# Wide cross-attention: a slot's order rewritten on TensorE, ScalarE and VectorE

## The chip, the cores and the metric

The kernel runs on one core of one Trainium2 chip. The time is device microseconds (us) of one execution. PE is TensorE, DVE VectorE, ACT ScalarE, POOL GpSimd.

## The reference, cut to what matters

The whole kernel is a decoder of two layers over 64 batches of 128 rows of 128 numbers. The change lies in its second stage, the cross-attention of the first layer, and in the routing that this stage prepares for the sparse experts after it:

```
xn = layernorm(layernorm(x)) * gamma + beta
q = (xn @ w_q).reshape(B, 128, 16, 64)
k, v = split(ctx @ w_kv)            # 77 keys per batch, 16 heads of 64
attn = softmax(q * 64**-0.5 @ k.T)          # per head
x = x + ((attn @ v) @ w_out + b_out) * tanh(gate)
scores = layernorm(x) @ Wg.T                # 8 experts, the two best are taken
```

## The kernel before, in words

The query and key weights of each head are folded beforehand into one 128 x 128 matrix `x0_a`, so that a batch's scores are its normalised rows times (`x0_a` times its context). Products that need more precision are made in three matmuls from a high and a low part of each side (`products`, L754 to L758).

The stage (`cross_attention_wide`, L686) is a pipeline in slots, one batch more in each. `run_slots` (L52) writes slots 0 to 23 out, runs 24 to 63 as a loop of five turns of eight slots, and writes 64 to 80 out. Each engine has its own `slot` function, whose order is written out by hand; engines meet through semaphores only. In slot t, the lag of a step says which batch it works on: `SCORE` 4 works on batch t - 4, `WEIGH` 5, `VALUE` 6, `LAST` 7, `TURN` 2, `ROUTE` 11, `RANK` 15, `PLACE` 16, `SCATTER` 17.

What each part does:

- Key products (`projected`): each slot makes the products of four heads (n = 0 to 3) for four batches at once, 4 x 77 = 308 columns each; four slots make all sixteen heads. PE writes to a bank of PSUM (`ps_u`), ACT copies the high part (L895), DVE subtracts to get the low part (L1060), and then the bank is free. n uses bank n % 2.
- Scores (`scores`): twelve matmuls fill `ps_s`. DVE takes the maxima (L1129) and subtracts them (L1135), ACT takes the exponent (L936), DVE sums and inverts (L1119, L1122), POOL normalises (`x_p`, L1013).
- `transposes`: PE turns the normalised weights, 16 heads in four groups (L816), into `ps_s`; ACT copies each group to `pT` (L912).
- `values`: the context times the value weights, in two halves of 512 columns (L756 to L758 into `ps_u`), copied by ACT to `v` (L919).
- `outputs`: weights times values, in two halves of eight heads (L803). Each head fills 64 of the 128 rows of the bank `ps_o`; ACT copies a half to `oT` (L903) before the second half may write the same bank.
- Sums (L850): `oT` times the output weights; DVE adds them to x (L1148) and takes statistics (L1150). POOL adds the bias (L1039) and, every fourth slot, turns four batches' statistics into mean and rate (`scalars`, L968 to L993). In that slot it waits for the statistics ahead of the bias (L1030).
- Routing: x is scaled (L1142), turned (L873), multiplied with the router (L838). Every fourth slot DVE ranks four batches (`rank`, L1077 to L1096, a chain of twelve small instructions), PE counts them (L881, L884), DVE works out rows (`place`, L1098 to L1112), and POOL scatters two rows per slot by indirect DMA (L1044).

PE's order in a slot before: scores; key products 0 and 1; router; outputs, half 0; sums; key products 2 and 3; outputs, half 1; transposes of groups 0, 1; values, half 0; transposes 2, 3; values, half 1; the two turns; counts. DVE's: sum and reciprocal; maxima; low parts 0 and 1; subtraction of the maxima; scaled rows; addition and statistics; low parts 2 and 3; normalised rows; rank; place.

## Time and profile before

| | |
|---|---|
| median of 3 runs | 2955.29 us (2955.25 to 2963.03) |
| profiled execution | 2969.01 us, span 2967.2 us |
| mean granted clock of TensorE | 0.958 of full |
| PE busy, whole span | 2706.5 us (91%) |
| DVE, ACT, POOL busy | 2098.4 (71%), 1925.4 (65%), 1942.6 (65%) |
| one more batch in the loop | 467.1 us / 40 slots = 11.68 us |

Busy time is the time in which an engine's records run. PE's records of matmuls overlap, since matmuls are pipelined; the distance between two starts is what one costs. PEld is the load of weights, which has its own records and shows waits that the overlapping matmul records hide. "<-" names who released the engine; "issue" means that the profile shows nothing it waited for. Times of a timeline count from the start of the span.

### The profile page before, as it was taken

To read this page: it belongs to the slowest core of one execution; us is meant where nothing else is said; L and a number is where in the kernel's file an instruction comes from. 1 tells how busy PE (TensorE), PEld (TensorE's weight loads), DVE (VectorE), ACT (ScalarE), POOL (GpSimd) and SP (SyncE) were. 2 spreads that over 40 slices of the span, in tenths; PEclk is the share of its full clock that TensorE was granted. 3 is DMA by queue.
4 is the path that set the end of the run, shared out by engine and by line. 5 is a ranking of instruction groups with operands and counts; after the bars stand their busy time and mean duration, and the time that the engine had idled before them with its cause. 6 is when DMAs were issued, how large, how long until landed. Compare 5 with 4: busy or idle time off the path is not lost. (4 is left out here: it accounts for less than half of the span.)

```text
span 2967.2 us, 82354 instructions
## 1 busy us (share of the span) xinstructions
PE 2706.5 (91%) x27846; PEld 2302.1 (78%) x27847; DVE 2098.4 (71%) x4559; ACT 1925.4 (65%) x4348; POOL 1942.6 (65%) x3245
## 2 busy tenths in 40 slices
PE   7999996999999999679997999996799999999996
PEld 5788775888888888579996788884577777778775
DVE  4677654676677666456665999997878888888643
ACT  3666543666666666345553777775788888888762
POOL 4556543466666666615667898995668787777753
PEclk9999987999999999889998999997799999999999
DMA  8565640000000000023332000000000000000000
GB/s 238 181 182 180 183 123 20 1 7 13 13 12 14 13 12 14 25 96 87 88 88 75 1 0 0 0 0 1 1 1 5 9 5 9 5 9 5 9 5 11
DMA packets 204792, 129.08 MB, mean 44 GB/s; under 512 B 13840, under 2 KB 197112, under 8 KB 203896
## 3 DMA queue, kind: packets, MB, share of 16 engines
q1 hardware_dynamic: 196344, 108.80, 12.3%
q0 software_dynamic: 8192, 16.79, 1.9%
q8 instruction: 169, 2.77, 0.4%
q14 instruction: 87, 0.71, 0.1%
HBM read 35.05 MB, written 90.51 MB: 42 GB/s over the span
## 5 line engine op out<-in xcount | busy, mean ns | idle before, releaser
L1575 PE MATMUL a_ps_s<-a_qk,w_ident 128*128 128x256 f32 x1024 | 237.7, 386 | 21.1 <-POOL a_qk L1682 20.0
L1013 POOL TENSOR_TENSOR x_p<-x_p,x_rz 128x1232 f32<-128x1232 f32 x64 | 143.9, 2248 | 166.3 <-DVE x_rz L1122 165.3
L635 DVE TENSOR_REDUCE a_nmax<-a_ps_s 128x4 f32<-128x512 f32 x256 | 165.0, 686 | 113.3 <-PE a_ps_s L381 109.7
L479 ACT ACTIVATE a_e<-a_ps_s 128x512 f32<-128x512 f32 x256 | 138.9, 595 | 156.6 <-PE a_ps_s L386 156.6
L1682 POOL TENSOR_TENSOR a_qk<-a_qkv 128x2048 f32<-128x2048 f32 x64 | 235.6, 3681 | 2.6 <-POOL a_eight L218 1.0
L2427 POOL TENSOR_TENSOR x_sq<-x_e 128x1232 f32<-128x1232 f32 x64 | 143.3, 2239 | 140.2 <-DVE x_t_sq L2590 140.1
L1575 PEld LDWEIGHTS a_ps_s<-a_qk,w_ident 128*128 128x128 f32 x1024 | 191.4, 192 | 51.0 <-POOL a_qk L1682 23.6
L1656 ACT ACTIVATE a_r<-a_o,w_a_rows 128x128 f32<-128x128 f32 x512 | 220.7, 521 | 2.4 <-DVE a_o L1741 1.6
L1411 POOL DMA_INDIRECT f_yg<-f_rows_out,f_index x120 | 115.0, 958 | 135.0 <-DVE f_yo L1490 114.8
L895 ACT ACTIVATE x_uu_hi<-x_ps_u 128x308 fp32r<-128x308 f32 x256 | 101.7, 423 | 108.4 <-PE x_ps_u L758 108.2
L1129 DVE TENSOR_REDUCE x_top<-x_ps_s 128x16 f32<-128x1232 f32 x64 | 91.2, 1425 | 111.7 <-PE x_ps_s L758 111.7
L381 PE MATMUL a_ps_s<-a_k_bd,a_q 32*128 32x128 f32 x2048 | 152.3, 287 | 9.4 <-issue 5.9
L2278 ACT ACTIVATE x_pT<-x_ps_s 77x512 f32<-77x512 f32 x256 | 140.1, 594 | 22.1 <-PE x_ps_s L2154 22.1
L386 PE MATMUL a_ps_s<-a_q,a_k_bd 32*128 32x128 f32 x2048 | 150.1, 284 | 2.0 <-issue 2.0
L2154 PE MATMUL x_ps_s<-w_ident,x_d 128*77 128x128 f32 x1024 | 147.5, 283 | 3.3 <-DVE x_d L2573 3.1
L2408 POOL TENSOR_TENSOR x_d<-x_d,x_g 128x1232 f32<-128x1232 f32 x64 | 144.0, 2249 | 10.0 <-ACT x_g L2365 10.0
L1727 DVE TENSOR_TENSOR a_ev<-a_ps_e,a_qkv 128x2048 f32<-128x2048 f32 x64 | 146.2, 2285 | 6.0 <-ACT a_ps_e L1664 4.7
L1044 POOL DMA_INDIRECT f_rows_in<-f_xr,f_where x120 | 121.0, 1009 | 39.5 <-issue 28.9
L1595 PEld LDWEIGHTS a_ps_y<-w_a_o,a_r 128*128 128x128 f32 x1024 | 127.2, 196 | 25.2 <-issue 9.3
L2154 PEld LDWEIGHTS x_ps_s<-w_ident,x_d 128*77 128x77 f32 x1024 | 124.7, 154 | 26.1 <-issue 19.8
L1060 DVE TENSOR_TENSOR x_uu_lo<-x_ps_u,x_uu_hi 128x308 fp32r<-128x308 f32 x256 | 110.6, 472 | 45.5 <-ACT x_uu_hi L895 45.4
L936 ACT ACTIVATE x_p<-x_p 128x1232 f32<-128x1232 f32 x64 | 78.9, 1233 | 97.8 <-DVE x_p L1135 97.8
(629 smaller groups left out, 9719.8 us busy)
## 6 DMA issues: line engine op xcount, KB each, us to landing
f_rows_in<-a_zeros SPq DMA_DIRECT2D x31, 1088.0 KB, 5.4
f_rows_out<-a_zeros SPq DMA_DIRECT2D x31, 1088.0 KB, 8.8
f_xin<-f_rows_in SPq DMA_DIRECT2D x135, 64.0 KB
f_rows_out<-f_yo SPq DMA_DIRECT2D x135, 64.0 KB
out<-x SPq DMA_DIRECT2D x16, 256.0 KB, 2.3
f_raw<-in_late_f SPq DMA_DIRECT2D x2, 1408.0 KB, 6.4
w_ctx<-in_ctx SPq DMA_DIRECT2D x1, 2464.0 KB
f_rows_in<-f_xr,f_where POOLq DMA_INDIRECT x128, 2.3
```

The lines of the kernel that those rows point to most:

```text
L381: nat = nc.tensor.matmul(ps_s[g][:, j * P:j * P + P], q[strip(g), u, :], k_bd[strip(g), u, j, :], start=False, stop=j == GROUP - 1)
L386: turned = nc.tensor.matmul(ps_s[g][:, j * P:j * P + P], k_bd[strip(g), u, j, :], q[strip(g), u, :], start=False, stop=j == GROUP - 1)
L635: nc.vector.tensor_reduce(nmax[:, u % 2, g, :], ps_s[g][:, :].rearrange("p (t k) -> p t k", t=GROUP), AX.X, ALU.max, negate=True).then_inc ...
L1013: nc.gpsimd.tensor_tensor(wide, wide, rz[:, :].unsqueeze(2).broadcast_to([P, HEADS, K]), ALU.mult).then_inc(p_ready, 1)
L1575: ins = nc.tensor.matmul(ps_s[u % 2][:, 0:HEADS * HEADS], c.ident[:, :], qk[:, u % 2, k, :, :], start=k == 0, stop=k == HD - 1)
L1656: ins = nc.scalar.activation(r[:, u % 2, :, :, a], o[:, u % 2, :, :].rearrange("p h d -> p d h"), ACT.Copy, scale=c.w["a1_rows"][:, a:a + 1])
L1682: nc.gpsimd.tensor_tensor(qk[:, u % 2, :, :, :], qkv[:, u % UNROLL, 0, :, :].unsqueeze(3).broadcast_to(full), qkv[:, u % UNROLL, 1, :, :]. ...
L1727: nc.vector.tensor_tensor(ev[:, u % 2, :, :, :], weights_of(u).unsqueeze(2).broadcast_to(n), qkv[:, u, 2, :, :].unsqueeze(1).broadcast_to( ...
L2154: ins = nc.tensor.transpose(ps_s[0:K, r, j * P:j * P + P], d[:, spread % RING, r, j, :], c.ident[:, :])
L2278: nc.scalar.activation(pT[:, GROUP * r:GROUP * r + GROUP, :], ps_s[0:K, r, :].rearrange("p (j q) -> p j q", j=GROUP), ACT.Copy).then_inc(p ...
L2408: nc.gpsimd.tensor_tensor(wide, wide, g[:, a, b, :].unsqueeze(2).broadcast_to([P, HEADS, K]), ALU.mult).then_inc(dg_ready, 1)
L2427: nc.gpsimd.tensor_tensor(sq[:, :, :], e[:, s % 2, :, :], e[:, s % 2, :, :], ALU.mult).then_inc(sq_ready, 1)
```

## The change

PE's new order in a slot: scores; sums; router; outputs, both halves; key products 0 and 1; transposes 0, 1; key products 2 and 3; transposes 2, 3; the two turns; counts; values, both halves. The second output half gets the bank that was `ps_o`, the first half writes to `ps_u[0]`; key products use `ps_u[1], ps_u[0], ps_u[1], ps_u[0]` for n = 0 to 3, values `ps_u[1], ps_u[0]`. ACT follows this order, with the exponent behind the last copy of `pT`. DVE subtracts the maxima directly behind taking them, then does the first half of the rank chain, `place` (a slot later than before), low parts 0 and 1, scaled rows, addition and statistics, normalised rows, low parts 2 and 3, and the second half of the rank chain. Waits that others imply are left out in the loop. POOL's code is unchanged.

```diff
+        ps_o = [ps_u[0], ps_one]
+        bank_of = [ps_u[1], ps_u[0], ps_u[1], ps_u[0]]
...
@@ PE, scores
-                wait(pe, d_ready, s)
-                pe.wait_ge(u_ready, 4 * (s - u % 4 + 4))
+                if fixed:
+                    wait(pe, d_ready, s)
+                if fixed or u % 4 == 0:
+                    pe.wait_ge(u_ready, 4 * (s - u % 4 + 4))
...
@@ PE, sums (new function summed), its waits
+                pe.wait_ge(oT_ready, 2 * (s + 1))
+                turned, routed = s + LAST - TURN, s + LAST - ROUTE
+                wait(pe, xT_ready, min(turned, B) if fixed else turned)
+                wait(pe, rT_ready, routed)
...
@@ PE, outputs
                 if half == 0:
-                    pe.wait_ge(pT_ready, (s + 1) * 4)
+                    if fixed:
+                        pe.wait_ge(pT_ready, (s + 1) * 4)
                     pe.wait_ge(v_ready, 2 * (s + 1))
-                wait(pe, oT_ready, 2 * s + half)
+                elif fixed:
+                    wait(pe, oT_ready, 2 * s)
...
@@ PE, key products
+                if n >= 2:
+                    pe.wait_ge(u_ready, 4 * s + n - 1)
+                elif fixed and s < VALUE:
+                    wait(pe, u_ready, 4 * s - 1 + n)
+                elif n == 1:
+                    pe.wait_ge(oT_ready, 2 * (s - VALUE) + 1)
+                elif fixed:
+                    pe.wait_ge(v_ready, 2 * (s - VALUE) + 1)
+                products(bank_of[n][:, 0:W], ...)
...
@@ PE, slot
                 if at := sl.step(SCORE):
-                    scores(at)
-                if at := sl.step(0):
-                    projected(at, (0, 1))
+                    scores(at, sl.fixed)
+                if at := sl.step(LAST):
+                    summed(at, sl.fixed)
                 if at := sl.step(ROUTE + 1):
+                    routed(at, sl.fixed)
                 if valued:
-                    outputs(valued, 0)
+                    outputs(valued, sl.fixed, 0)
+                    outputs(valued, sl.fixed, 1)
+                if at0:
+                    projected(at0, sl.fixed, 0)
+                    projected(at0, sl.fixed, 1)
                 if spread:
-                    transposes(spread, (0, 1))
-                    values(spread, 0)
-                    transposes(spread, (2, 3))
-                    values(spread, 1)
+                    transposes(spread, sl.fixed, (0, 1))
+                if at0:
+                    projected(at0, sl.fixed, 2)
+                    projected(at0, sl.fixed, 3)
+                if spread:
+                    transposes(spread, sl.fixed, (2, 3))
...
+                if spread:
+                    values(spread, sl.fixed, 0)
+                    values(spread, sl.fixed, 1)
...
@@ ACT, slot
-                if at := sl.step(0):
-                    projected(at, (0, 1))
...
                 if valued:
                     outputs(valued, 0)
+                    outputs(valued, 1)
+                if at0:
+                    projected(at0, (0, 1))
+                if spread:
+                    transposed(spread, (0, 1))
+                if at0:
+                    projected(at0, (2, 3))
+                if spread:
+                    transposed(spread, (2, 3))
                 if at := sl.step(SCORE):
...
@@ DVE, slot
...
-                if at := sl.step(0):
-                    projected(at, (0, 1))
...
+                if ranked:
+                    first_best(ranked)
+                if (at := sl.step(PLACE + 1)) and at[1] % BATCHES == 0:
+                    place(at)
+                if at0:
+                    projected(at0, (0, 1))
...
                 if at := sl.step(LAST):
                     dve.wait_ge(y_ps, s + 1)
+                    wait(dve, r_ready, s + LAST - ROUTE)
...
-                if at := sl.step(0):
-                    projected(at, (2, 3))
...
-                if (at := sl.step(RANK)) and at[1] % BATCHES == 0:
-                    rank(at)
-                if (at := sl.step(PLACE)) and at[1] % BATCHES == 0:
-                    place(at)
+                if at0:
+                    projected(at0, (2, 3))
+                if ranked:
+                    second_best(ranked)
```

`first_best` is the chain's first six instructions (the best expert and the scores without it), `second_best` the other six.

## Rows read from the trace of the kernel before

**Rows 1.** Busy us of each engine, TensorE clock, DMA share, in the loop's window

```profile
707.00:1174.00 467.00, 452.06 (x4003) 403.35 (x4001) 324.75 (x682) 304.44 (x650) 306.46 (x519) 1.00 0.04 13
```

**Rows 2.** Waits of weight loads, 571 to 1174: us in total, times, longest

```profile
PEld x_ps_u L756 <- DVE x_uu_lo L1060: 10.5, 16, 0.9
PEld x_ps_o L803 <- issue: 9.4, 52, 0.2
...
PEld x_ps_s L756 <- issue: 7.5, 4, 2.1
PEld x_ps_u L756 <- issue: 4.6, 8, 0.8
```

**Rows 3.** Timeline of PE, slot 26: start, us, instruction, count

```profile
731.13 0.39 PE L756 MATMUL x_ps_s<-x_uu_hi,x_x_hi 128*128 128x308 f32 x1
...
733.75 0.28 PE L838 MATMUL x_ps_misc<-w_f_router,x_rT 128*128 128x8 f32 x2
...
734.99 2.05 PE L850 MATMUL x_ps_misc<-x_o,x_oT 128*128 128x128 f32 x16
736.80 0.39 PE L756 MATMUL x_ps_u<-x_keys_hi,x_a_hi 128*128 128x308 f32 x1
...
737.82 1.09 PE L803 MATMUL x_ps_o<-x_pT,x_v 77*64 77x128 f32 x16
738.85 1.10 PE L816 MATMUL x_ps_s<-w_ident,x_p 128*77 128x128 f32 x8
...
742.18 0.38 PE L756 MATMUL x_ps_s<-x_uu_hi,x_x_hi 128*128 128x308 f32 x1
```

**Rows 4.** Timeline of PE, first scores of slots 24 and 64

```profile
706.88 0.39 PE L756 MATMUL x_ps_s<-x_uu_hi,x_x_hi 128*128 128x308 f32 x1
...
1173.97 0.39 PE L756 MATMUL x_ps_s<-x_uu_hi,x_x_hi 128*128 128x308 f32 x1
```

**Rows 5.** Timeline of DVE, slot 26

```profile
733.11 1.44 DVE L1129 TENSOR_REDUCE x_top<-x_ps_s 128x16 f32<-128x1232 f32 x1 [2.24 <-PE x_ps_s L758]
...
735.24 1.43 DVE L1135 TENSOR_TENSOR x_p<-x_ps_s,x_top 128x1232 f32<-128x1232 f32 x1
736.58 0.34 DVE L1142 TENSOR_SCALAR f_xr<-x,mean,rstd 128x128 f32 x1
...
737.61 0.29 DVE L1150 BATCH_NORM_STATS2 stats<-x  x1
738.28 0.86 DVE L1060 TENSOR_TENSOR x_uu_lo<-x_ps_u,x_uu_hi 128x308 fp32r<-128x308 f32 x2 [0.37 <-ACT x_uu_hi L895]
...
739.31 1.43 DVE L1119 TENSOR_REDUCE x_z<-x_p 128x16 f32<-128x1232 f32 x1
740.78 0.25 DVE L1122 RECIPROCAL x_rz<-x_z 128x16 f32<-128x16 f32 x1
```

**Rows 6.** Timeline of ACT, slot 26

```profile
733.53 0.85 ACT L895 ACTIVATE x_uu_hi<-x_ps_u 128x308 fp32r<-128x308 f32 x2 [1.23 <-PE x_ps_u L758]
...
736.70 1.23 ACT L936 ACTIVATE x_p<-x_p 128x1232 f32<-128x1232 f32 x1 [1.00 <-DVE x_p L1135]
...
739.54 1.08 ACT L912 ACTIVATE x_pT<-x_ps_s 77x512 f32<-77x512 f32 x2
```

**Rows 7.** Timeline of POOL, slots 26 and 27

```profile
738.18 0.45 POOL L1039 TENSOR_TENSOR x<-x,x_b 128x128 f32 x1 [3.00 <-DVE stats L1150]
...
741.20 0.21 POOL L981 TENSOR_TENSOR x_st<-stats 128x4 f32 x1
...
746.03 2.25 POOL L1013 TENSOR_TENSOR x_p<-x_p,x_rz 128x1232 f32<-128x1232 f32 x1
```

**Rows 8.** Timelines of DVE and POOL at the start of slot 24

```profile
706.58 0.19 DVE L1086 TENSOR_TENSOR x_eq<-x_rest,f_weight 128x32 f32<-128x32 f32 x1
706.88 0.51 DVE L1087 TENSOR_TENSOR x_pr<-x_eq,w_x_order 128x32 f32<-128x32 f32 x1
...
706.65 0.69 POOL L1003 TENSOR_TENSOR x_keys_hi<-x_raw,powers 128x308 fp32r<-128x308 f32 x1 [0.15 <-POOL x_raw L1000]
```

More of the change, by code:

```diff
@@ new lines, in summed, with routed @@
+                for n in range(PAIRS):
+                    ins = nc.tensor.matmul(ps_y, oT[:, u % 2, n, :], c.x0_o[:, n, :], start=n == 0, stop=n == PAIRS - 1)
+                ins.then_inc(y_ps, 1)
+            def routed(at, fixed):
+                s, u = at
+                if fixed:
+                    pe.wait_ge(rT_ready, s + 1)
+                    if u % BATCHES == 1:
+                        wait(pe, pos_ready, s - 1)
+                nc.tensor.matmul(ps_r, rT[:, u % 2, :], c.w["f0_router"][:, :],
+                                 start=True, stop=True).then_inc(r_ps, 1)
@@ L802, in outputs, with projected, transposes @@
                         h = half * PAIRS + 2 * n + odd
-                        ins = nc.tensor.matmul(ps_o[DH * odd:DH * odd + DH, n * P:n * P + P], v[:, u % 2, h * DH:h * DH + DH],
+                        ins = nc.tensor.matmul(ps_o[half][DH * odd:DH * odd + DH, n * P:n * P + P], v[:, u % 2, h * DH:h * DH + DH],
                                                pT[:, u % 2, h, :], start=True, stop=True)
                 ins.then_inc(o_ps, 1)
-            def transposes(at, groups):
+            def projected(at, fixed, n):
+                s, u = at
+                if n == 0 and (fixed or u % 4 == 0):
+                    pe.wait_ge(keys_lo_ready, s - u % 4 + 4)
+                if n >= 2:
[6 more added lines that the diff above has]
+                    pe.wait_ge(v_ready, 2 * (s - VALUE) + 1)
+                products(bank_of[n][:, 0:W], [t[:, 4 * (u % 4) + n, :] for t in c.x0_a], [t[:, u // 4, :, :] for t in keys], u_ps)
+            def transposes(at, fixed, groups):
                 s, u = at
@@ L817, in transposes, with values @@
                     ins.then_inc(pT_ps, 1)
-            def values(at, half):
+            def values(at, fixed, half):
                 s, u = at
-                pe.wait_ge(cx_lo_ready, s + 1)
-                done = 4 * (s + WEIGH + 1) - 1 + half
-                pe.wait_ge(u_ready, min(done, 4 * B) if sl_fixed(at) else done)
-                wait(pe, v_ready, 2 * (s - 1) + half + 1)
-                products(ps_u[half][0:K, :], [t[:, u % 2, :] for t in cx], [t[:, half * 512:half * 512 + 512] for t in c.x0_v], v_ps)
+                if half == 0:
+                    pe.wait_ge(cx_lo_ready, s + 1)
+                done = 4 * (s + WEIGH) + 3 + half
+                pe.wait_ge(u_ready, min(done, 4 * B) if fixed else done)
+                if fixed:
+                    wait(pe, oT_ready if half else v_ready, 2 * (s - 1) + 1)
+                products(bank_of[half][0:K, :], [t[:, u % 2, :] for t in cx], [t[:, half * 512:half * 512 + 512] for t in c.x0_v], v_ps)
@@ L840, in slot @@
-                if valued:
-                    outputs(valued, 0)
-                if at := sl.step(LAST):
-                    s, u = at
-                    wait(pe, r_ready, s + LAST - ROUTE)
-                    pe.wait_ge(oT_ready, 2 * (s + 1))
-                    turned = s + LAST - TURN
-                    wait(pe, xT_ready, min(turned, B) if sl.fixed else turned)
-                    wait(pe, x_done, s)
-                    for n in range(PAIRS):
-                        ins = nc.tensor.matmul(ps_y, oT[:, u % 2, n, :], c.x0_o[:, n, :], start=n == 0, stop=n == PAIRS - 1)
-                    ins.then_inc(y_ps, 1)
@@ L962, in slot @@
                     nc.scalar.activation(ranks[:, :, :], ps_rank, ACT.Copy).then_inc(pos_ready, BATCHES)
+                if spread:
+                    values(spread, 0)
+                    values(spread, 1)
             run_slots(act, slot, B, LAG, BODY)
@@ L1065, in _, with chained @@
             dve.wait_ge(opened, 1)
[L1067 to L1069 removed]
+            def chained(sem, each, s, begun=0):
+                n = [begun * BATCHES]
                 def after(ins):
@@ L1075, in chained, with best, first_best @@
                 return after
-            def rank(at):
+            def best(after, score, chosen, value):
+                order = c.w["x0_order"][:, :].unsqueeze(1).broadcast_to(tall)
+                after(nc.vector.tensor_reduce(value, score, AX.X, ALU.max))
+                after(nc.vector.tensor_tensor(eq[:, :, :], score, value.unsqueeze(2).broadcast_to(tall), ALU.is_equal))
+                after(nc.vector.tensor_tensor(pr[:, :, :], eq[:, :, :], order, ALU.mult))
+                after(nc.vector.tensor_reduce(lead[:, :], pr[:, :, :], AX.X, ALU.max))
+                after(nc.vector.tensor_tensor(chosen[:, :, :], pr[:, :, :], lead[:, :].unsqueeze(2).broadcast_to(tall), ALU.is_equal))
+            def first_best(at):
                 s, u = at
@@ L1114, in slot @@
             def slot(sl):
+                at0 = sl.step(0)
+                ranked = at if (at := sl.step(RANK)) and at[1] % BATCHES == 0 else None
                 if at := sl.step(WEIGH):
```

97 lines of the change are left out of this document (37 added, 60 removed).

## Prediction

> **What bounds the kernel now.** The stage that is changed runs from 466 us to about 1260 us of the profiled execution. I read the busy time by window first: over the 467 us of its loop, PE is busy 452.06 us at full granted clock, and no other engine is busy for more than 325 [rows 1]. So the stage goes at PE's pace, and time can come only from PE's own work or from PE's waits. Next, the waits of the weight loads, which show gaps that the pipelined matmul records cover: over 603 us they waited 10.5 us for DVE's low parts (L1060), 7.5 us in four pieces of "issue", 4.6 us more of issue ahead of a key product, and 9.4 us of issue ahead of the outputs (L803) in 52 pieces of about 0.18 each [rows 2].
>
> Then one undisturbed slot, matmul by matmul [rows 3]. It lasts 742.18 - 731.13 = 11.05 us. Twelve scores and six key products take 733.75 - 731.13 = 2.62, so 0.14 to 0.15 each, with no gap where one kind follows the other. Sixteen sums (L850) take 736.80 - 734.99 = 1.81: 0.11 each, the pace of transposes too. From 738.85 to 742.18 stand 16 transposes, two small products at that pace and six value matmuls: (3.33 - 1.98) / 6 = 0.23 each. An output group (L803) takes 1.03 until the next kind starts, although its 8 pairs at 0.11 are 0.87 (the records end after 0.85 of loads). Six key products and the change to the outputs take 737.82 - 736.80 = 1.02 instead of 0.84. So each output group costs about 0.17 on the way in and 0.15 on the way out, and a slot has two such groups.
>
> The loop's 40 slots take 1173.97 - 706.88 = 467.1 us, 11.68 each [rows 4]. That is 25 us over 40 quiet slots: four pauses, ten rank-count products of 0.29, and waits for low parts and for POOL's key split.
>
> **The change, part by part.** Let t be the slot's number, 0 its first score matmul, and call slots with t mod 4 = 0, 1, 2, 3 the mask, place, rated and rank slot.
>
> *Both output halves in one run.* One way in and one way out disappear: 0.17 + 0.15 = 0.32 us. Batches 0 to 63 each have a second half, so 64 x 0.32 = -20.5 us. The quiet slot becomes 11.05 - 0.32 = 10.73. Bounds: nothing, if the second half in its other bank keeps its gaps; 0.36 (0.18 of load wait [rows 2] each way), -23. I take 0.32.
>
> [...] Had the gap been the cost of the waits ahead of each group, it would stay on the way out.
>
> *The new slot on PE,* laid out at those paces: scores to 1.70; sixteen sums to 3.49; router and gap (1.24 from 733.75 to 734.99, less an output group) to 3.70; outputs to 5.49, gap to 5.69; products 0 and 1 to 6.54; eight transposes to 7.41; products 2 and 3 to 8.26; transposes to 9.13; the two small ones to 9.35; values to 10.73. Now each crossing to another engine has a due time.
>
> *DVE's first half.* The exponent moves behind the last copies of pT on ACT. Copies of pT take about 0.5 apart, key copies 0.3 to 0.43 [rows 6]; the last transpose leaves at 9.0, its copy runs from 9.4, the exponent from 9.9, and 1.23 long it ends at 11.1, which is 0.4 in the next slot. Sum 1.47 (740.78 - 739.31), reciprocal 0.25, maxima 1.44, subtraction 1.34 (736.58 - 735.24) [rows 5] end at 4.9 to 5.0. POOL's normalising starts at 2.3 and ends at 4.55, 2.25 long [rows 7]. The transposes need both at 6.54: 1.5 us in hand. So what is taken from between maxima and subtraction costs nothing.
>
> *Key products behind the maxima.* Product 2 reuses the bank of product 0 and waits for low part 0. Product 0's last matmul starts at 5.97, ends 0.30 later, ACT copies it (0.85 for two [rows 6]: 0.43) and DVE subtracts (0.86 for two less 0.39 of overlap: 0.47 [rows 5]): about 7.29 with three handoffs, against a due time of 7.41. Product 3 has the same 0.12 in hand. Then DVE does four small instructions of 0.29 to 0.34 [rows 5], starting 0.25 to 0.42 apart, so low part 2 starts at 8.7 to 8.9 and ends at 9.15 to 9.37; the first value matmul wants it at 9.35. I charge 3 us for the stage; the bounds are nothing and 0.35 in each of the 57 slots from 7 to 63, 20 us.
>
> *The old waits.* The rank chain and placing stood at the end of DVE's slot and made the next slot's low parts late; that is the 10.5 us. The other 4.6 are key products standing behind POOL's key split at 1.7 in the mask slot; now the first is due at 5.69. Both go: -15 us. Placing comes one slot later and no longer waits for ACT's copy of the ranks. Its eight instructions at 0.19, the ordinary length of such a one [rows 8], are 1.5 us and fit between 5.0 and 6.8. The rank chain's second half fits behind low part 3, which no PE step of that slot then awaits.
>
> *A new wait.* In the rated slot POOL waits for the statistics before its bias, two scatters and a chain of 13 small instructions; the next batch's normalising is queued behind all of them. Today statistics start at 6.48 in the slot (737.61); POOL starts 0.28 after they end, its small chain 3.02 later (741.20 - 738.18), normalising 4.83 after that (746.03), and it is done at 17.15, 6.10 in the next slot, where the transposes come at 7.7 [rows 3, 5, 7]. After the change the statistics stand behind low parts 0 and 1, which start 6.8 and 7.2, then the scaled rows and the addition: start 8.3, end 8.6. Then 8.6 + 0.28 + 3.02 + 4.8 + 2.25 = 18.95, or 8.2 in the rank slot, where PE wants it at 6.54. PE loses about 1.6. It happens once scatters run: rank slots 19 to 63, 12 x 1.6 = +19 us. Bounds 0.8 and 2.4 per rank slot (early statistics and short gaps; a late addition): +10 and +29. POOL's code is unchanged, so no part of this is bought back.
>
> *The rest.* At the start, the first exponent goes behind products 2 and 3, and nothing hides it: +1.5 (0 to 3). PE's loop end: four pauses, 7.5 us; values now stand last and queue without a blocking wait, -1 (0 to -4). Placing one slot later at the end of the stage, beside scatters: 0 to +1.
>
> *Sum:* -20.5 - 15 + 19 + 3 + 1.5 - 1 = -13 us. The profiled execution took 2969.0 us with a span of 2967.2, so about 2956 and 2954; the median of the runs shown lies 13.7 lower than the profiled time, so 2955.3 - 13 = **2942 us**.
>
> **A rule against the new order.** With DVE's rank chain beside POOL's key split, L1087 took 0.51 us where L1086 before it took 0.19, and ended as POOL's L1003 did (707.39 and 707.34) [rows 8]. In the new rank slot the chain's first half (from 4.9) meets normalising (from 5.95 to 8.2). Held until 8.2, it would have low part 0 ready at 9.4, and product 2, behind transposes that end at 9.1, would lose 0.3: 12 x 0.3 = +4 us.
>
> [...]
>
> **Rivals.**
> 1. *Forecast:* joined outputs pay, the statistics wait takes most of the rest: -6 to -20 us, 2935 to 2949, chance 0.47.
> 2. *POOL is not late,* because statistics or the addition come early: half or less of the 19: -23 to -33, 2922 to 2932. For it: POOL has 1.6 in hand today. Against it: code order puts two low parts and the scaled rows ahead. 0.15.
> 3. *Low part 2 is late for the values in every slot:* 0.25 x 57 = 14 more: about +1, 2956. For it: 0 in hand against 0.2 of spread; against it: undisturbed starts are close together. 0.20.
> 4. *Other side: the ring of product 0, copy, low part 0, product 2.* Only 0.12 is in hand, and ACT must first have copied the outputs' second half, which starts at 5.7. Each further 0.1 costs 57 x 0.1 = 5.7 us. At 0.23 over the 0.12 the gain is gone; from 0.39 over it the kernel is slower by more than 9. At 0.5 over, -13 + 28 = +15: 2970. For it: three handoffs; against it: each copy's row is short and ACT is 65% busy. 0.10.
> 5. *The change doesn't do what it says:* the gaps stay with the two halves. -13 + 20 = +7: 2962. 0.08.
>
> **How the numbers follow.** The measurement tells 0.3%, about 9 us, from no change. Faster needs less than 2946.4: rival 2 (0.15) and about nine tenths of the forecast (0.43), with small parts of 3: 0.60. Same: the rest of the forecast, nearly all of rival 3, most of 5: 0.28. Slower: 0.12. The range reaches from rival 2's lower end to rival 5: 2922 to 2962, which leaves out rival 4 and the far ends. For the forecast alone it is 2935 to 2949.
>
> **What would show it.** In the trace after: quiet slots of 10.7 to 10.8; L803 in runs of 32 with one issue wait in and one out; rank slots about 12.3, with L816 waiting on POOL's L1013 by about 1.6; hardly any wait of value matmuls for L1060; key products in mask slots without issue waits. The prediction is wrong if L816 does not wait on L1013 (rival 2), if the value products or products 2 and 3 wait for L1060 in most slots (3, 4), or if a second gap stands inside the run of 32 (5).

## The result

Seven runs of the changed kernel have a median of 2931.87 us (2924.59 to 2942.17), seven of the kernel before 2955.61 (2954.12 to 2969.49). The ratio is 0.9903, with a 95% interval of 0.9882 to 0.9925, which is 22 to 35 us. The direction and the range were right; the gain is about twice the forecast's 13 us. Both kernels spread by some 15 us, and TensorE's granted clock in the first stage, which is not changed, is one part of it: in the profiled executions that stage ends at 465.8 us before, with a mean granted clock of 0.96 of full, and at 452.8 after, with 0.99. So what follows is read within the stage. From its first key product to its last scatter it took 803.8 us before and 777.2 after, **26.6 less**.

The windows of the loop after (us; then busy us and number of records for PE, PEld, DVE, ACT, POOL; clock, DMA share, GB/s), which answers to [rows 1]:

```profile
688.00:1138.00 450.00, 435.82 (x3999) 405.80 (x3998) 340.14 (x680) 306.78 (x651) 306.87 (x519) 1.00 0.04 12
```

PE does the same work in 17 us less, 16.2 of them busy time: the overlapping matmul records cover most gaps, so "busy" was no sign of work. The first scores of slots 24 and 64, for [rows 4]:

```profile
687.78 0.30 PE L758 MATMUL x_ps_s<-x_uu_hi,x_x_hi 128*128 128x308 f32 x1
...
1138.39 0.30 PE L758 MATMUL x_ps_s<-x_uu_hi,x_x_hi 128*128 128x308 f32 x1
```

40 slots take 450.6 us, 11.27 each. My terms give about 459: 467.1, less 40 x 0.32, 12 of old waits and 1 of pauses, plus 10 x 1.6 and 2. Slot 26 on PE, for [rows 3]:

```profile
709.55 0.30 PE L758 MATMUL x_ps_s<-x_uu_hi,x_x_hi 128*128 128x308 f32 x1
...
711.24 1.95 PE L801 MATMUL x_ps_misc<-x_o,x_oT 128*128 128x128 f32 x16
713.02 0.29 PE L810 MATMUL x_ps_misc<-w_f_router,x_rT 128*128 128x8 f32 x2
713.24 1.09 PE L824 MATMUL x_ps_u<-x_pT,x_v 77*64 77x128 f32 x16
714.17 1.04 PE L824 MATMUL x_ps_o<-x_pT,x_v 77*64 77x128 f32 x16
715.14 0.41 PE L758 MATMUL x_ps_u<-x_keys_hi,x_a_hi 128*128 128x308 f32 x1
...
720.30 0.30 PE L758 MATMUL x_ps_s<-x_uu_hi,x_x_hi 128*128 128x308 f32 x1
```

The slot takes 720.30 - 709.55 = 10.75 us (forecast 10.73). The two output halves are one run: the second starts 0.93 behind the first, eight pairs at 0.12 with no gap, and both with their way out take 714.17 + 0.97 - 713.24 = 1.90, where each of two took 1.03, and each had its own way in.

The waits of weight loads over the same slots as [rows 2] (552 to 1138 here; us in total, times, longest):

```profile
PEld x_ps_s L852 <- POOL x_p L1046: 19.1, 12, 1.8
PEld x_ps_u L758 <- issue: 9.5, 53, 0.6
PEld x_ps_u L758 <- DVE x_uu_lo L1093: 1.6, 3, 0.7
```

Four things are to be seen. The wait for low parts fell from 10.5 to 1.6. The new wait for POOL's normalising is there, 12 times 1.6, as forecast. The 53 waits of about 0.18 ahead of key products are the one way out of the outputs that is left; before, a slot had three such waits, those ahead of L803 in [rows 2] and these two, behind either half:

```profile
PEld x_ps_s L816 <- issue: 8.9, 52, 0.2
PEld x_ps_misc L850 <- issue: 8.9, 52, 0.2
```

And the "issue" wait of the scores in [rows 2], 7.5 us in four pieces, is gone altogether: I had taken 1 us off for it.

How the new wait comes about is in the rank slot 31 and the slot ahead of it. The timelines of DVE, POOL and PE, in order of time: DVE's statistics and POOL's bias behind them, then POOL's normalising with DVE's rank chain beside it, and PE's transposes:

```profile
763.06 0.29 DVE L1191 BATCH_NORM_STATS2 stats<-x  x1
763.63 0.46 POOL L1072 TENSOR_TENSOR x<-x,x_b 128x128 f32 x1 [2.41 <-DVE x_xn L1197]
771.21 0.19 DVE L1115 TENSOR_REDUCE x_lead<-x_pr 128x4 f32<-128x32 f32 x1
771.34 2.25 POOL L1046 TENSOR_TENSOR x_p<-x_p,x_rz 128x1232 f32<-128x1232 f32 x1
771.50 2.14 DVE L1116 TENSOR_TENSOR x_first_of<-x_pr,x_lead 128x32 f32<-128x32 f32 x1
773.64 1.10 PE L852 MATMUL x_ps_s<-w_ident,x_p 128*77 128x128 f32 x8 [1.39 <-POOL x_p L1046]
774.08 0.86 DVE L1093 TENSOR_TENSOR x_uu_lo<-x_ps_u,x_uu_hi 128x308 fp32r<-128x308 f32 x2
```

Statistics start 8.5 us into their slot (forecast 8.3). L1116, a 0.19 us instruction with two inputs, runs for 2.14 and ends when POOL's normalising does; low part 0 follows. PE was standing for the same POOL instruction, so this hold costs nothing yet.

### The profile page after: what moved, and what is told of

Same layout as the page of the kernel before. It is cut to its first block and busy times, and to the rows that moved or that the text cites. A ratio compares the mean times of both kernels' runs of the same rounds, so it can differ in the third digit from the quotient of the medians.

```text
span 2924.0 us, 81980 instructions
## 1 busy us (share of the span) xinstructions
PE 2670.0 (91%) x27846; PEld 2297.5 (79%) x27847; DVE 2118.5 (72%) x4559; ACT 1928.5 (66%) x4348; POOL 1943.4 (66%) x3245
## 3 DMA queue, kind: packets, MB, share of 16 engines
q1 hardware_dynamic: 196344, 108.80, 12.5%
## 5 line engine op out<-in xcount | busy, mean ns | idle before, releaser
L944 ACT ACTIVATE x_pT<-x_ps_s 77x512 f32<-77x512 f32 x256 | 137.7, 590 | 24.8 <-PE x_ps_s L852 24.0
L2317 ACT ACTIVATE x_pT<-x_ps_s 77x512 f32<-77x512 f32 x256 | 140.0, 594 | 21.0 <-PE x_ps_s L2193 20.6
L1157 DVE TENSOR_REDUCE x_z<-x_p 128x16 f32<-128x1232 f32 x64 | 91.9, 1436 | 84.1 <-ACT x_p L975 82.2
L852 PE MATMUL x_ps_s<-w_ident,x_p 128*77 128x128 f32 x1024 | 133.8, 275 | 20.1 <-POOL x_p L1046 17.4
L1634 PEld LDWEIGHTS a_ps_y<-w_a_o,a_r 128*128 128x128 f32 x1024 | 125.5, 194 | 26.5 <-issue 10.1
```

Source lines behind the costliest of these rows:

```text
L2317: nc.scalar.activation(pT[:, GROUP * r:GROUP * r + GROUP, :], ps_s[0:K, r, :].rearrange("p (j q) -> p j q", j=GROUP), ACT.Copy).then_inc(p ...
```

## The experiments

Durations of slots are distances between first score loads in the trace. Ratios are to executions of the kernel before on the same chip; where none is given there is one execution, and the text goes by its slots. A quiet slot takes 11.05 to 11.08 before and 10.73 to 10.78 after, a rank slot 12.5 to 12.7 after, and a mask slot 11.0 after.

A long slot is not always a wait. In the 40 slots of before and of the changed kernel TensorE's granted clock stays at the upper of its two levels, 1.00 of full, throughout, and so it does in all three runs with early statistics and in the one with the whole rank chain put back. In others it falls to the lower, 0.50, for stretches of 3.4 us (a few are twice as long), always in or behind a pause or a wait of PE: 3.6 us long and 0.4 ahead of 788.0 with 37 extra waits per slot; the shortest single wait is the 1.65 ahead of 777.3 with nine. The windows of two mask slots behind a pause, in the changed kernel moved by 120 instructions (columns as above; the clock is the third number from the end):

```profile
793.00:796.30 3.30, 3.30 (x17) 3.30 (x16) 1.77 (x2) 0.00 (x0) 2.96 (x7) 0.50 0.00 0
1079.00:1083.00 4.00, 4.00 (x48) 3.98 (x48) 2.84 (x2) 0.18 (x1) 3.61 (x8) 1.00 0.02 4
```

The first slot takes 12.7 us, the second 11.1. One stretch of 3.4 us makes a slot 1.4 to 1.9 us longer.

### What took the loop's four pauses away

Before, the record of PE's branch back to the loop's start takes 3.6 to 4.1 us; after, 0.22. PE executes 1780 instructions per turn of eight slots before and 1706 after, since the change leaves out waits. Theory 1: the length of the body. Theory 2: the new order, values last with no blocking wait. Two waits share one record: 19 extra waits per slot make a turn 72 records longer (1778 against 1706), 9 per slot.

**All loop waits back in the changed kernel** (one of the dozen places):

```diff
-                if fixed:
-                    wait(pe, r_ready, routed - 1)
-                    wait(pe, x_done, s)
+                wait(pe, r_ready, routed - 1)
+                wait(pe, x_done, s)
```

> The changed kernel with every wait of PE's loop put back that the change had dropped there as implied (they are all satisfied when PE comes to them), so that PE has about as many instructions per loop turn as before (some 1780 instead of 1706). Theory 1 (the four pauses of before at PE's loop ends come from the length of PE's loop body): the pauses return, the record of PE's branch takes 3.6 to 4.1 us again instead of 0.22, and the 40 slots from slot 24 to 64 take 450.6 + 7.5 = 458 us. Theory 2 (the pauses vanished because the values stand last and PE runs ahead through the end of the loop without a blocking wait): nothing of the order is changed here, but more waits stand in the way, so a part of the pauses may return, 0 to 7.5 us. My forecast's own step (the pauses stay nearly as they are whatever the count) is already refuted by the profile after.

**19 satisfied waits more per slot, and 9:**

```diff
+            def filler(fixed, n):
+                if not fixed:
+                    for k in range(n):
+                        pe.wait_ge(fill[k % 6], 1 + k // 6)
...
+                filler(sl.fixed, 7)
```

> The changed kernel with 19 extra waits per slot in PE's loop, each on a value that a semaphore passed long ago and so never blocking: PE's loop turn gets 152 instructions more and the order and every blocking wait stay as in the changed kernel. Theory 1 (length of the loop body): the pauses return, PE's branch record takes 3.6 to 4.1 us, the slots 24 to 64 take about 458 us instead of 450.6. Theory 2 (no blocking wait at the loop's end): no pause, 450.6 to 452. That waits cost PE's sequencer time by themselves would show in the slots that are no loop ends, as more than 10.8 us in a quiet slot.

> As the run with 19 extra waits per slot, with 9: a body about half-way between the changed kernel's and the one before. Theory 1 with a threshold: either no pause at all or four whole ones (450.6 or about 458 us for slots 24 to 64); a pause that grows with the length would give about half, 454 us. Theory 2: 450.6 to 452.

**The kernel before, its implied loop waits left out** (as in the change, order untouched):

```diff
-                wait(pe, v_ready, 2 * (s - 1) + half + 1)
+                if sl_fixed(at):
+                    wait(pe, v_ready, 2 * (s - 1) + half + 1)
```

> The kernel before, in its own order, with implied waits left out of PE's loop, so that a turn has some 264 instructions less than before's. Theory 1 (length of the loop body): the four issue pauses ahead of the first scores vanish, slots 24 to 64 take 467.1 - 7.5 = 459.6 us, and the kernel is about 7 us faster than before (ratio 0.9975). Theory 2 (the order and its blocking waits make the pauses): they stay, 467.1, ratio 1.000.

Measured: before's order with 1747 records (33 fewer, not the 264 of the expectation) has no pause, takes 461.2 instead of 467.1 for the 40 slots, and is faster: ratio 0.9976 (0.9958 to 0.9994). So the pauses cost 5.9 us net, since the mask slots behind them were 0.4 shorter. 1737 records in the changed order: no pause. 1778: four. But 1780 with the waits back: none. Neither theory explains that pair. Closer to the limit:

```diff
-                filler(sl.fixed, 6)
+                filler(sl.fixed, 4 if at0 and at0[1] % 2 else 6)
```

> The run with 19 extra satisfied waits per slot (1778 records, 14 fused, it paused: slots 24 to 64 took 14 us more than the changed kernel's), now with two of them left out in every second slot: 1774 records, 14 fused. Theory 1a (length with fused records counted twice, limit between 1789 and 1792): 1788, no pause, slots 24 to 64 at about 451. Rival (position or timing of the extra waits decides): the pauses stay, 464.

> The changed kernel with all waits back in PE's loop, and 4 satisfied waits more per turn: 1784 instruction records per turn, of which 9 are fused pairs of register operations. So far turns of 1780 (12 fused; before) and of 1778 (14 fused; 19 extra waits per slot) pause, and turns of 1780 (9 fused; all waits back) and less don't. Theory 1a (length decides, and a fused record counts for two: the limit lies above 1789 and at or below 1792): this turn counts 1793 and pauses, a branch record of 3.5 to 5 us and 40 slots in about 458 instead of 450.6. Rival (where the extra waits stand or the timing at the loop's end decides, not the length): no pause, since the four waits stand early in a slot and the rest is as in the run without a pause.

One pause in four at 1774, two in four at 1784. The refinement of counting fused records twice is refuted by the first. Then far above the limit, a little below before's length, and the odd one again:

> The changed kernel with 37 satisfied extra waits per slot: 1850 instruction records per turn of PE's loop, well above the band of 1774 to 1784 in which turns have paused or not. Theory 1 (length of the loop body): all four branches back pause, records of 3.5 to 5 us. Rival (the order of the changed kernel avoids the pause and what paused were other effects): not all four. Extra waits also cost PE's sequencer some time of its own; a quiet slot beyond 10.8 would show that.

> The kernel before in its own order with only ten instruction records less per turn of PE's loop (1770 instead of 1780; three kinds of implied waits left out). Theory 1 (length, with a band between about 1750 and 1785 in which chance decides): fewer than four pauses, none or one, slots 24 to 64 at 459.6 to 462. Rival (before's order makes the pause): four pauses, 467.

> The changed kernel with all loop waits back (1780 records), the same as in the first call, where none of its four branches paused. If chance decides in the band, this execution may show one to four pauses, as the neighbours at 1774 and 1784 did; if something of this code decides (its waits are on registers, the fillers' on constants), none again.

1850 records pause each time; before's order pauses each time at 1770, where I had expected at most one; the 1780 with the waits back again never does. Length alone is refuted. A third theory: the place of the body in the code. Both ways, with an untouched loop. By place I forecast pauses at all four branches of the changed loop, 3.5 to 5 us each, and 458 to 466 for slots 24 to 64; for before's loop with ten records less no pause, branch records of 0.22 and 459.6 to 462. Which lengths pass at which place was my guess:

```diff
+                if sl.fixed and sl.t == 9:
+                    padding(240)
```

> The changed kernel, its loop untouched (1706 instruction records per turn), with 120 instructions that only wait for long satisfied semaphores in one slot ahead of the loop, so that the loop's code lies 120 instructions later. [...] Theory 1 (length) and theory 2 (order): no pause, 450.6. [...]

> The kernel before with ten instructions less per turn (1770, as in the run where all four branches paused), its loop moved by 228 instructions by satisfied waits in one slot ahead of it. [...] Theories 1 and 2 (length, order): four pauses of 4.4 to 4.7 us again, 470.

The changed kernel's own 1706 instructions, 120 further back in the code, pause at all four branches (the waits of weight loads of that run; L758 has no such row in the changed kernel):

```profile
PEld x_ps_s L758 <- issue: 13.5, 4, 3.6
```

PE at the end of its first turn, the last value matmul and the first of the scores:

```profile
788.49 0.40 PE L760 MATMUL x_ps_u<-x_v_hi,x_cx_lo 128*77 128x512 f32 x1
791.83 0.40 PE L758 MATMUL x_ps_s<-x_uu_hi,x_x_hi 128*128 128x308 f32 x1 [2.94 <-issue]
```

In the changed kernel those two stand 0.23 apart. And before's order with 1770 records, which paused at every branch, loses all its pauses when it is moved by 228 (its last turn and its first scores):

```profile
818.11 0.27 PE L886 MATMUL x_ps_misc<-w_ident,f_xr 128*128 128x128 f32 x1
818.14 0.39 PE L756 MATMUL x_ps_s<-x_uu_hi,x_x_hi 128*128 128x308 f32 x1
```

| kernel | records per turn | branches that paused | slots 24 to 64, us | of these at clock 0.50, us |
|---|---|---|---|---|
| before | 1780 | 4 of 4 | 467.1 | 0 |
| before, ten fewer | 1770 | 4 of 4 | 478.4 | 17.1 |
| before, ten fewer, moved by 228 | 1770 | 0 of 4 | 461.4 | 0 |
| before, implied waits out | 1747 | 0 of 4 | 461.2 | 0 |
| changed | 1706 | 0 of 4 | 450.6 | 0 |
| changed, moved by 120 | 1706 | 4 of 4 | 469.8 | 13.7 |
| changed, 9 extra waits per slot | 1737 | 0 of 4 | 453.4 | 6.8 |
| changed, 19, thinned | 1774 | 1 of 4 | 458.1 | 3.4 |
| changed, 19 extra waits per slot | 1778 | 4 of 4 | 473.4 | 17.1 |
| changed, waits back (two runs) | 1780 | 0 of 8 | 452.2, 450.6 | 3.4, 0 |
| changed, waits back and 4 more | 1784 | 2 of 4 | 463.2 | 6.8 |
| changed, 37 extra waits per slot | 1850 | 4 of 4 | 469.1 | 13.7 |

What follows: length and place together decide whether the branch pauses, and the order doesn't protect. The waits that the change leaves out are enough to end the pauses in before's order (1747), but the changed order doesn't need it: with all of them back at 1780 it has no pause in eight branches. At the unlucky place the changed kernel's loop is 19.2 us slower, which is slower than before's. A paused slot takes 15.3 to 15.8 there instead of 12.5, 3.1 for each pause. The rest is clock: behind three of the four pauses it falls, and the mask slot takes 12.7 instead of 11.0, and once more in a rank slot that takes 14.0. In before's order the four pauses cost 467.1 - 461.2 = 5.9 us at full clock, and 478.4 - 461.4 = 17.0 with ten records less, where the clock is at its lower level for 17.1 us; half of that, 8.5, is my estimate of the clock's part.

The body of before begins 11 instructions later than the changed one (1000 instructions that only wait stand ahead of it in PE's trace, against 989). Counted from where the changed body begins, the bodies at these two places that end at 1706 to 1758 don't pause, those that end at 1774 to 1784 went either way (1, 4, 0, 4 and 2 branches of four, the 0 twice), and those that end at 1791 and 1850 pause each time. The body moved by 120 ends at 1826 and pauses, the one moved by 228 begins at 239, ends at 2009 and doesn't. The forecasts by place came true in the number of pauses; the changed loop took 469.8, above its 458 to 466. The runs show the effect of place; what PE does in a pause, what decides between 1774 and 1784, and why the third place is free of pauses, they don't show.

### The joined outputs

**The router product between the halves again, on PE and ACT:**

```diff
+                if valued:
+                    outputs(valued, sl.fixed, 0)
                 if at := sl.step(ROUTE + 1):
                     routed(at, sl.fixed)
                 if valued:
-                    outputs(valued, sl.fixed, 0)
                     outputs(valued, sl.fixed, 1)
```

> The changed kernel with the router product (one 128-row product with 8 columns) put between the two output halves on PE, and its copy between their copies on ACT: the run of 32 output matmuls is cut into two of 16, with full-width work between, as before; everything else stays, and the number of instructions too. My forecast's term (a way in of 0.17 and a way out of 0.15 for each run of output matmuls): every slot that has a router product between its halves, 53 of them, costs 0.32 more, so a quiet slot of 11.07 to 11.10 instead of 10.75 to 10.78, and slots 24 to 64 take 450.6 + 40 x 0.32 less what the rank slots hide in their wait for POOL (10 x 0.32) = about 460. Rival (the gaps belong to the two halves or to their waits, whatever stands between them; the joining itself brought nothing): quiet slots stay at 10.75.

Quiet slots take 11.09 to 11.12 (three are longer), 0.35 more: the gaps belong to the two runs of 64-row work, as the forecast had it. But slots 24 to 64 take 478.9, not 460, and the ratio to before is 0.9999 (0.9985 to 1.0012): the whole gain is gone. Rank slots took 13.3 to 13.6 in five cases and 15.2 to 15.3 in the other five. The timelines of POOL and DVE in the rank slot 31:

```profile
782.03 2.25 POOL L1048 TENSOR_TENSOR x_p<-x_p,x_rz 128x1232 f32<-128x1232 f32 x1
782.07 0.19 DVE L1114 TENSOR_REDUCE f_weight<-x_sc 128x32 f32 x1 [0.95 <-ACT x_sc L963]
782.36 1.97 DVE L1115 TENSOR_TENSOR x_eq<-x_sc,f_weight 128x32 f32<-128x32 f32 x1
```

ACT copies the router's scores later, so the rank chain starts 0.95 late and its second instruction meets the whole of POOL's normalising. The hold that cost nothing in the changed kernel now stands ahead of low part 0 with four instructions still to come. PE waits 1.30 us for POOL in this slot and then 1.17 for low part 0. The slots of 15.2 have the same waits; in all five the granted clock falls to 0.50 behind them (slot 39, with slot 31 beside it):

```profile
788.00:791.00 3.00, 3.00 (x21) 2.53 (x20) 2.25 (x8) 3.00 (x6) 2.54 (x4) 1.00 0.13 44
880.93:884.30 3.37, 3.37 (x17) 3.18 (x16) 2.71 (x11) 2.08 (x5) 2.91 (x4) 0.50 0.12 39
```

This kernel can't price the joining in a rank slot; a later one does.

### The wait for POOL

**Addition and statistics of the rated slot directly behind the subtraction:**

```diff
+                last = sl.step(LAST)
+                early = last and last[1] % BATCHES == BATCHES - 1
+                if early:
+                    added(last)
                 if ranked:
                     first_best(ranked)
```

> The changed kernel with DVE's addition and statistics of the rated slot (t mod 4 = 2) put directly behind the subtraction of the maxima instead of behind two low parts and the scaled rows. My forecast's mechanism (the statistics are late for POOL's bias, scatters and chain, and with them the next normalising): statistics end about 3 us earlier, the normalising in the rank slot ends before the transposes come for it, the waits of the transposes for POOL (20.8 us in 14 waits in the changed kernel's profile) go to nearly nothing, a rank slot takes 10.8 to 11.2 instead of 12.5 to 12.7, slots 24 to 64 about 434 to 437, the kernel about 20 us less than the changed one: 2912, ratio to before 0.984. Rival 1 (POOL is late by its own work, the scatters and the small chain, not by the statistics' place): the wait moves by less than 3 us but its size stays, 2930. Rival 2 (the ring of product 0, copy, low part 0, product 2 has nothing to spare, and two more instructions ahead of it make it late in the rated slot): the rated slot grows by 0.3 to 0.6 and gives back 4 to 8 us.

The mechanism is right: 1.8 us of waits for POOL's `x_p` over the whole stage instead of 20.8, ratio to before 0.9858 (0.9838 to 0.9878). The size is not: slots 24 to 64 take 444.5, not 434 to 437, and rank slots 11.7 to 12.2. What was hidden behind the wait for POOL came out (waits of weight loads, and DVE in the rank slot that begins at 764.13):

```profile
PEld x_ps_u L758 <- DVE x_uu_lo L1093: 10.1, 12, 1.0
```

```profile
769.46 1.05 DVE L1113 TENSOR_TENSOR x_eq<-x_sc,f_weight 128x32 f32<-128x32 f32 x1
...
772.02 0.86 DVE L1093 TENSOR_TENSOR x_uu_lo<-x_ps_u,x_uu_hi 128x308 fp32r<-128x308 f32 x2
```

Half a chain, one instruction of it held, puts low part 0 at 7.9 in the slot, and product 2 waits 0.9 for its bank.

**Two of those six instructions moved behind low part 3:**

```diff
+            EARLY = 4
+                best(chained(own, 11, s), sc[:, u // BATCHES, :, :], top1, c.f0_weight[:, 0, bass.ds(s, BATCHES)], (0, EARLY))
...
+                after = chained(own, 11, s, EARLY)
+                best(after, sc[:, u // BATCHES, :, :], top1, c.f0_weight[:, 0, bass.ds(s, BATCHES)], (EARLY, 5))
```

> The run with the early statistics, and its first half of the rank chain cut once more: four instructions behind the subtraction as before, the other two (the choice's comparison and the masking) moved behind low part 3, in front of the second half. Theory (in the run with the early statistics the rank slots still take 11.7 to 12.2 us instead of 10.8, since the six instructions, one of them held by POOL's normalising, delay low part 0 by about 0.9 us): low part 0 starts at about 7.3 in the rank slot instead of 7.9, the rank slot takes 11.0 to 11.4, slots 24 to 64 lose 10 x 0.6 = 6 us against that run's 443, the kernel 7 us, ratio to before 0.983. Rival (low part 0 is late because POOL holds whatever DVE does beside its normalising, not because of the number of instructions): the next instructions with two inputs are held in the same way and the rank slot stays at 11.7; ratio 0.986. A second rival: the two moved instructions make the next slot's sum late, which gives 0.6 back in each mask slot: no change in the sum.

Low part 0 starts at 7.2, rank slots take 10.9 to 11.0, mask slots stay at 11.0, slots 24 to 64 take 435.9 (the first rank and one mask slot are 0.4 longer). The ratio to before is 0.9849 (0.9827 to 0.9872); the stage takes 756.4 us in the profile, against 767.0 with the early statistics alone, 777.2 in the changed kernel and 803.8 before. Its waits for low parts, which were 10.1:

```profile
PEld x_ps_u L758 <- DVE x_uu_lo L1093: 1.4, 5, 0.6
```

This is the fastest version of the stage; over the whole kernel its interval overlaps with that of the early statistics alone. All three have the same 1706 instructions per turn, no pause, and full clock in the 40 slots.

**The same, with the router product between the halves:**

> The run with early statistics and the chain cut in three, now with the router product between the two output halves on PE and ACT, as in the first run that undid the joining. That first run lost 28 us in slots 24 to 64 where the joining accounts for 40 x 0.35 = 14: its rank slots took 13.3 and 15.2 us instead of 12.5. Theory (two separate things: 0.35 per slot for the second way in and out, and in rank slots the later copy of the router's scores, which starts the chain 0.65 to 0.95 later, into POOL's normalising of 2.25 us, which holds one of its instructions for 2 us and with it low part 0): here POOL's normalising is nearly over when the chain starts and only four instructions stand ahead of low part 0, so only the 0.35 is left: quiet slots 11.1, rank slots 11.2 to 11.5, slots 24 to 64 at 435.9 + 14 to 17 = 450 to 453, ratio to before about 0.991. Rival (the surplus comes from the router product's place itself, through the ring of product 0, its copy and low part 0): the rank slots again take 13 us or more and slots 24 to 64 some 463.

Quiet slots 11.09 to 11.14, rank slots 11.1 to 11.4, slots 24 to 64 at 448.5, ratio 0.9909 (0.9893 to 0.9926). The clock is full here too, so the joining is worth 12.6 us over 40 slots, 0.32 each. The first run's surplus of 14 us is not all the late chain, as the theory had it: some 9 us of it stand in the five slots in which the clock falls, each 1.6 to 1.9 longer than the others, and the rest is the wait for low part 0 (0.8 to 1.2 in a rank slot, less 0.35 by which the wait for POOL is shorter). That the clock fell because of the two waits behind each other fits (without the late chain it doesn't fall), but slot 31 has the same waits and keeps its clock.

### The other two parts

**The whole rank chain and the placing back at the end of DVE's slot:**

```diff
-                if ranked:
-                    first_best(ranked)
-                if (at := sl.step(PLACE + 1)) and at[1] % BATCHES == 0:
-                    place(at)
...
+                if ranked:
+                    first_best(ranked)
+                    second_best(ranked)
```

> The changed kernel with the whole rank chain (and the placing, a slot earlier again) at the end of DVE's slot, as before the change; all else as changed. My forecast's term (chain and placing at the end of DVE's slot made the next slot's low parts late: 10.5 us of waits before the change): with subtraction and low parts now behind each other, the mask and place slots lose 0.7 to 1.0 us each, about 10 to 20 us for the stage, and the rank slots, which wait for POOL anyway, gain nothing while POOL is late. Slots 24 to 64: 457 to 467 instead of 450.6. Rival (the split of the chain brings nothing in the new order; low parts have enough room behind the subtraction): 449 to 452.

466.3 us for the 40 slots, 15.7 more than the changed kernel, and in the profile this row:

```profile
PEld x_ps_s L852 <- POOL x_p L1046: 39.6, 27, 1.9
```

The size is the expected one, the way is another: not the low parts but the next slot's sum is late, and through it the reciprocal and POOL's normalising. Mask slots take 12.2 to 12.9.

**Low parts 0 and 1 between maxima and subtraction:**

```diff
+                if at0:
+                    projected(at0, (0, 1))
                     dve.wait_ge(max_done, s + 1)
                     nc.vector.tensor_tensor(p[:, u % 2, :, :, :], data, each.unsqueeze(3).broadcast_to([P, GROUPS, GROUP, K]),
```

> The changed kernel with low parts 0 and 1 between the maxima and the subtraction again, as before the change; PE's and ACT's order stay as changed. PE now makes key products 0 and 1 only at 5.7 to 6.5 in a slot, so DVE waits for them with the subtraction behind. My working (the subtraction must follow the maxima in the new order): low part 0 starts at 6.9, the subtraction at 8.2 to 8.6 and ends near 10, the exponent and low parts 2 and 3 are late, and PE's values wait for these: a slot takes 12.5 to 14 instead of 10.75, slots 24 to 64 510 us or more. Rival (there is enough room, the move on DVE is not needed): 10.75 to 11.

Slots of 13.4 and more, slots 24 to 64 at 556.7; for 27.3 us of these the clock is at 0.50, an estimated 14 us, so the move itself is worth over 90. The move is a condition of PE's new order and not a gain by itself. The wait is not where I put it, at the values:

```profile
PEld x_ps_s L852 <- issue: 139.4, 52, 2.7
```

It is the transposes, which write the bank that the subtraction has to read first; PE's own record in the slot that begins at 836.66 has 2.47 us there for DVE's subtraction.

## Why the prediction was half right

By its own steps, in the profiled executions:

- **Both output halves in one run**, -20.5 at 0.32 a slot: right. Quiet slots fell by 0.31, and two kernels that differ in nothing else differ by 0.32.
- **The old waits**, -15: right in kind and too small. 10.5 became 1.6 and the issue waits of key products in mask slots are gone. But I charged 12 us for the 40 slots from the wait rows, and the lengths of slots say 16: against before without its pauses (the run with implied waits out), place slots lost 1.38 and mask slots 0.84, of which the joining explains 0.31 each. With slots 17, 20, 21 and 65 it is 19 for the stage. With the chain whole again the loop loses 15.7 us, though by another way.
- **The new wait for POOL**, +19: right in place and number, and nearly in size (12 in [rows 2]'s stretch, 1.6 each; 20.8 for the stage). Rank slots grew by a little more, 1.8 beyond the joining, which makes 23. The early statistics remove it.
- **Low parts late for product 2 and the values**, +3: none. The 0.12 us in hand held, and 1.6 us in three waits is all there is.
- **The end of PE's loop**, -1 out of "0 to -4": the step that failed most. 7.5 us of pauses vanished, worth 5.9 net. I charged -1 because values now stand last and queue without a blocking wait, so as if the order covered a part of a pause that stays. The runs show that the pause depends on where the body's code lies and how long it is, and not on the order (1706 records pause at none of four branches at their own place and at all four 120 later); what PE does in it they don't show. The text names "four pauses, 7.5 us" twice and gives no reason for them.
- **The start**, +1.5: -3. From the first scores to slot 6 the stage takes 1.2 less, at the lower clock for the same part of it (10.7 us, and 10.5 before). I feared for the exponent behind products 2 and 3. But in slot 5 the transposes wait for the subtraction, which the change brings forward: they begin 6.4 us after the slot's first scores instead of 7.8. Another 1.9 went between the first key product and the first scores, and what took it is open; all runs with the changed order take 17.4 to 18.5 us there, and those with before's 19.4 to 20.4.
- **The end of the stage**, 0 to +1 for the placing: from slot 64 to the last count 78.2 became 74.0, of which some 2 us are joined outputs and 0.8 an old wait for POOL in slot 65; in slot 67 a new one of 1.5 goes the other way.

Put right, the sum is -20 (joining) - 19 (old waits) + 23 (POOL) + 1 (slot 15, 0.5 longer beside the joining's 0.3) - 3 (start) - 6 (pauses) = -24, against 26.6 measured in the stage. The missing 2 to 3 us lie behind slot 64 and are not told apart. So in the forecast's miss of 26.6 - 13 = 13.6 us the pauses are 5, the start 4 to 5, the old waits 4 and the low parts 3, and POOL's term goes 4 the other way, a part that cancels by luck. The **rule against the new order** that I weighed is borne out by the trace (L1116 held for 2.14 us), but the charge of 4 us was not paid here, since PE was waiting for the same POOL instruction. The sum left it out and was right to, though the prediction gives no reason: it works the hold and the wait for POOL out apart and never asks whether they fall together. Once that wait was gone, low part 0 was late for 10.1 us, by the hold (1.05 in the slot shown) and by the number of instructions ahead of it.

## What to carry to other kernels

An "issue" wait at a loop's end that stands at one place per turn can be a matter of the code's size and place: count the instructions of the body in both kernels, and before crediting an edit, try the same loop moved by a hundred instructions. When one wait on an engine is removed, list what ran in its shadow; here a held instruction and half a chain came out behind it, and cutting the chain was worth as much as moving the statistics. Before a long slot is put down to a wait, read the granted clock in it. A part of a change that moves a small instruction can cost many times its own time when its follower meets a long instruction of another engine: the router product, 0.28 us, in another place let an instruction of 0.19 run for 1.97.

## What the runs showed of the hardware

- A branch back in PE's loop takes 0.21 to 0.24 us or 3.4 to 5.1. The changed loop goes from 0.22 up to 3.4 to 3.9 when its code lies 120 instructions later, and before's with ten fewer from 4.4 to 4.7 down to 0.21 when it lies 228 later.
- Instructions on PE that only wait, each for two satisfied semaphores, take 0.11 us each in a row (116 of the 120 that move the changed loop take 12.7 us, from 518.26 to 530.93); with the clock that falls there (0.50 from 523.3 to 537.0, and from 537.0 to 560.9 with 228), 120 cost two slots 15 us and 228 cost 25. Spread over the matmuls of a slot, nine and even eighteen such instructions cost nothing (quiet slots stay at 10.75).
- A DVE instruction of 0.19 us with two inputs ran for 1.97 and 2.14 us beside POOL's normalising; the reductions beside it kept their 0.19, and the subtraction, whose large input lies in PSUM, its 1.44. An instruction with one large input was long beside it too: in the kernel before, the scaled rows (L1142, 0.34 us in [rows 5]) took 1.20 us at 1207.77 and ended 0.08 behind POOL's normalising.
- The granted clock of TensorE falls from 1.00 to 0.50 of full for 3.4 us in single slots behind a pause of 3 us, behind waits of 1.3 and 1.2, or in or behind a wait of 1.65 or 1.8, and not in all slots with such waits: behind three of four pauses in one run, behind none in the kernel before, and behind none of the changed kernel's ten waits of 1.6 to 1.8 in the 40 slots.
